# Apply stage of a split-precision block product: high and low columns in one 512-column matmul

## The reference

```python
h   = x @ weight.T + bias1 + scale[adapter] * (x @ A[adapter].T) @ B[adapter].T   # rank 16
Wq  = NF4[codes] * absmax           # one absmax per block of 64
out = x + h @ Wq.T + bias2
```

## Time and profile before

| | |
|---|---|
| median of 3 runs | 2300.09 us (2298.8 to 2300.9) |
| profiled execution, its own time | 2299.26 us |
| its span in the trace | 2297.5 us |
| PE busy, PEld busy | 2202.1 us (96%), 2009.1 us (87%) |
| DVE, ACT busy | 1707.1 us (74%), 1116.0 us (49%) |
| DMA, mean | 240 GB/s |
| apply stage, matmuls L1076, L1077, L1078 on comb,xs | 3584 each |

### The profile page before, as it was taken

The page is one execution under the profiler, slowest core; times in us unless marked ns, Lnnn a source line. Parts: engine busy times, 40 slices in busy tenths (PEclk is TensorE's granted clock), DMA queues, the critical chain, the costliest instruction groups (busy, mean ns, idle before and its releaser), DMA issues.

```text
span 2297.5 us, 37544 instructions
## 1 busy us (share of the span) xinstructions
PE 2202.1 (96%) x15082; PEld 2009.1 (87%) x15082; DVE 1707.1 (74%) x2434; ACT 1116.0 (49%) x1494; POOL 0.2 (0%) x4
## 2 busy tenths in 40 slices
PE   1489999999999999999999999999999999999999
PEld 1368877887788777899999999999999999999999
DVE  8988897897888565487777776676776676767665
ACT  6666665665666333354444443433444343443432
POOL 0000000000000000000000000000000000000000
PEclk9799999999999999999999999999999999999999
DMA  5248887887787898877777877777887777977775
GB/s 116 73 147 259 253 272 217 269 253 229 252 262 244 252 302 271 262 244 236 241 234 233 273 266 244 239 239 248 283 265 239 238 243 244 303 249 235 242 244 171
DMA packets 399331, 550.51 MB, mean 240 GB/s; under 512 B 41624, under 2 KB 256280, under 8 KB 399032
## 3 DMA queue, kind: packets, MB, share of 16 engines
q1 hardware_dynamic: 399160, 548.12, 76.0%
HBM read 421.66 MB, written 127.42 MB: 239 GB/s over the span
## 4 chain that ended last, share of the span: by engine, by line
PE 57%; DVE 0%; issue 0%; DVEq 0%
PE ps L1078 18%; PE ps L1076 18%; PE ps L1077 18%; PE ps L1119 1%; PE ps L1108 0%; DVE xs L870 0%; DVE res L949 0%; DVE res L927 0%; DVE res L942 0%; DVE low_st L887 0%; DVE low_rep L934 0%; DVEq L947 0%
## 5 line engine op out<-in xcount | busy, mean ns | idle before, releaser
L1076 PE MATMUL ps<-comb,xs 128*128 128x256 f32 (+1 forms) x3584 | 1014.6, 283 | 1.7 <-issue 1.0
L1078 PE MATMUL ps<-comb,xs 128*128 128x256 f32 (+1 forms) x3584 | 1014.6, 283 | 0.0
L1077 PE MATMUL ps<-comb,xs 128*128 128x256 f32 (+1 forms) x3584 | 1009.3, 282 | 0.0
L611 ACT CAST xs<-xr 128x1024 fp32r<-128x1024 f32 x427 | 448.1, 1051 | 633.2 <-DMA xr<-xc_d 632.7
L870 DVE TENSOR_TENSOR xs<-xr,xs 128x1024 fp32r<-128x1024 f32 x427 | 522.3, 1224 | 293.6 <-ACT xs L611 291.7
L1077 PEld LDWEIGHTS ps<-comb,xs 128*128 128x128 f32 x3584 | 677.8, 189 | 5.3
L1076 PEld LDWEIGHTS ps<-comb,xs 128*128 128x128 f32 x3584 | 676.6, 189 | 2.3 <-issue 1.4
L1078 PEld LDWEIGHTS ps<-comb,xs 128*128 128x128 f32 x3584 | 676.7, 189 | 0.0
L1076 PE MATMUL ps<-wq,tile 128*128 128x512 f32 x1088 | 476.1, 438 | 0.0
L1078 PE MATMUL ps<-wq,tile 128*128 128x512 f32 x1088 | 427.7, 393 | 0.0
L1077 PE MATMUL ps<-wq,tile 128*128 128x512 f32 x1088 | 426.7, 392 | 0.0
(11 more groups left out here) (99 smaller groups left out, 1720.2 us busy)
## 6 DMA issues: line engine op xcount, KB each, us to landing
xr<-xc_d SPq DMA_DIRECT2D x427, 512.0 KB, 4.0
raw<-in_L_cond_weight_dram SPq DMA_DIRECT2D x128, 512.0 KB, 4.6
xc_d<-rq SPq DMA_DIRECT2D x32, 1792.0 KB, 7.6
x_nat<-in_x_dram SPq DMA_DIRECT2D x128, 256.0 KB, 3.8
res<-in_x_dram SPq DMA_DIRECT2D x64, 512.0 KB, 5.4
out_dram<-res SPq DMA_DIRECT2D x128, 256.0 KB, 5.0
wc_d<-cs SPq DMA_DIRECT2D x32, 896.0 KB, 4.6
comb_raw<-wc_d SPq DMA_DIRECT2D x28, 1024.0 KB, 7.4
```

The source lines that it names most:

```text
L611: nc.scalar.copy(xs[f][:, HI, :, :], xr[f][:, LO, :, :]).then_inc(s_xhi, 1)
L1076: nc.tensor.matmul(out_ap, t_hi, m_hi, start=first, stop=False)
L1077: nc.tensor.matmul(out_ap, t_hi, m_lo, start=False, stop=False)
L1078: return nc.tensor.matmul(out_ap, t_lo, m_hi, start=False, stop=last)
```

## The change

A predicate is_wide(i) names the products that are done in another form. In strip 0 these are SS1, S4 and A22 of passes 0 to 14; in strips 1 to 3 all seven products, without those of the last pass of strips 1 and 2 and without the first two of each strip's first pass. (The last pass of strip 0 is out as well; the last of strip 3 is in.)

For such a product the high part of x is multiplied in one matmul with the high and the low columns of the weight block, 2x256 columns, into the whole bank. The low part of x is multiplied with the high columns as before, into the left half. So a step of k has two matmuls (512 and 256 columns) instead of three (256 each). In the last step the two change places, so that the 512-column matmul is the last of the product. The right half of the bank then holds x high by weight low, and DVE adds it in an instruction of its own ahead of the old one, with a wait of DVE for itself (s_evh) in between. The other products keep their form.

```diff
+    def is_wide(i):
+        pp, f = divmod(i, NF)
+        j, p = divmod(pp, PAIRS)
+        if p == PAIRS - 1 and j + 1 < NS:
+            return False
+        return f not in WITH_LOW if j == 0 else not (p == 0 and f < 2)
+
+    def wide_before(i):
+        return sum(is_wide(n) for n in range(i))
...
+                wide, n_wide = is_wide(i), wide_before(i) + 1
+                low_half = bank[:, HW:2 * HW]
                 if f == A11:
+                    if wide:
+                        tt(u_sum[:, :], low_half, u_sum[:, :], ALU.add).then_inc(s_evh, 1)
+                        dve.wait_ge(s_evh, n_wide)
                     tt(r[:, 0, 0, :], u_sum[:, :], r[:, 0, 0, :], ALU.add).then_inc(s_ev, 1)
...
                 elif f == SS1:
+                    if wide:
+                        tt(r[:, :, 1, :], low_half.unsqueeze(1).to_broadcast([P, 2, HW]), r[:, :, 1, :],
+                           ALU.add).then_inc(s_evh, 1)
+                        dve.wait_ge(s_evh, n_wide)
                     tt(r[:, :, 1, :], bank[:, 0:HW].unsqueeze(1).to_broadcast([P, 2, HW]), r[:, :, 1, :],
                        ALU.add).then_inc(s_ev, 1)
...
-                for k in range(HK):
+                if is_wide(i):
+                    for k in range(HK):
+                        x_hi, x_lo = xs[f][:, HI, k, :], xs[f][:, LO, k, :]
+                        both, high = cw[f][:, k, :, cols], cw[f][:, k, HI, cols]
+                        if k < HK - 1:
+                            nc.tensor.matmul(bank[:, :], x_hi, both, start=(k == 0), stop=False)
+                            nc.tensor.matmul(bank[:, 0:HW], x_lo, high, start=False, stop=False)
+                        else:
+                            nc.tensor.matmul(bank[:, 0:HW], x_lo, high, start=False, stop=False)
+                            last = nc.tensor.matmul(bank[:, :], x_hi, both, start=False, stop=True)
+                    last.then_inc(s_prod, 1)
+                for k in range(0 if is_wide(i) else HK):
                     last = three(psum, xs[f][:, HI, k, :], xs[f][:, LO, k, :], cw[f][:, k, HI, cols],
                                  cw[f][:, k, LO, cols], k == 0, k == HK - 1)
```

More of the change, by code:

```diff
@@ L264, in adaln_ffn_kernel @@
         s_ev = sem("product_added")
+        s_evh = sem("high_columns_of_wide_product_added")
         s_ab = sem("a_b_loaded")
@@ L918, in add_product @@
                         tt(spread(0), thrice(u_low[:, :]), thrice(bank[:, low]), ALU.add).then_inc(s_lrep, 1)
+                    if wide:
+                        tt(r[:, 0, 0, :], low_half, r[:, 0, 0, :], ALU.add).then_inc(s_evh, 1)
+                        dve.wait_ge(s_evh, n_wide)
                     tt(r[:, 0, 0, :], bank[:, main], r[:, 0, 0, :], ALU.add).then_inc(s_ev, 1)
@@ L939, in add_product @@
                 elif f == S4:
+                    if wide:
+                        tt(r[:, 0, 1, :], low_half, r[:, 0, 1, :], ALU.add).then_inc(s_evh, 1)
+                        dve.wait_ge(s_evh, n_wide)
                     tt(r[:, 0, 1, :], bank[:, 0:HW], r[:, 0, 1, :], ALU.add).then_inc(s_ev, 1)
                 else:
+                    if wide:
+                        tt(r[:, 1, 0, :], low_half, r[:, 1, 0, :], ALU.add).then_inc(s_evh, 1)
+                        dve.wait_ge(s_evh, n_wide)
                     tt(r[:, 1, 0, :], bank[:, 0:HW], r[:, 1, 0, :], ALU.add).then_inc(s_ev, 1)
@@ L1227, in _ @@
                 pe.wait_ge(s_xlo, split_of(i) + 1)
-                for k in range(HK):
+                if is_wide(i):
[10 more added lines that the diff above has]
+                for k in range(0 if is_wide(i) else HK):
                     last = three(psum, xs[f][:, HI, k, :], xs[f][:, LO, k, :], cw[f][:, k, HI, cols],
                                  cw[f][:, k, LO, cols], k == 0, k == HK - 1)
-                last.then_inc(s_prod, 1)
+                    if k == HK - 1:
+                        last.then_inc(s_prod, 1)
                 if j == 0 and f == 3:
```

## The result

The changed kernel takes 2285.83 us (median of 6 runs, 2283.67 to 2287.02), the kernel before 2299.64 us in the same comparison: a ratio of 0.9938, 95% interval 0.9928 to 0.9949. So it is faster by 14 us. 2271 us was forecast, with a range of 2264 to 2285: the direction was right, the size was twice too large, and the time lies just outside the range.

The account below looks back on a forecast made before the run. PE was taken to bound the apply stage, by number of matmuls times their distance. 2299.3 - 30.6 (PE steps) + 1.2 (strip starts) + 0.5 (end) = 2270.4, so 2271 us with the median's 0.8; range 2264 to 2285 us.

Parts of the forecast that it names:

- 226.7 + 118.7 = 345.4 ns: PE's step of k in wide products: one 512- and one 256-column matmul instead of 356.0 ns, saving 10.6 ns.
- The 118.7 ns: PE's distance for a 256-column matmul in the apply stage, worked out from a pass of 20.39 us.
- The end: After the last block matmul one more DVE add stands before L942: +0.5 us, all visible.
- DVE in mid-strip: DVE 86 to 90% busy in mid-strip, idle time ahead of L870 halved, at no cost to PE.
- The start of a strip: Late DVE adds at three strip starts: 0.5 us to spare before product 231; 0 to 6 us put, 1.2 taken.
- A: Rival: the dropped matmul was cheap, 512-column distance 230 to 235 ns, saving 7 to 21 us; 2281 to 2295 us; chance 0.08.
- A's sign: On PE, a 512-column distance over 232 ns would make the rival of the cheap dropped matmul true.
- a mean of 58 steps: End of the weight stage: 13.15 us / 58 = 226.7 ns, taken as the 512-column distance.
- B: Rival: PE waits for DVE at strip starts or x comes late, 4 to 8 us back each; 2280 to 2293; chance 0.09.
- C: Rival: DVE becomes the bound, a pass longer than 20.39 us, slower than before, for instance 2317 us; chance 0.04.
- D: Rival: the load was the true limit at 256 columns, so more gain than forecast, below 2265 us; chance 0.04.
- The rule of the Trainium skill: Matmul distance at full clock is columns / 2.4 plus 2.5 ns; one matmul less saves 2.5 ns a step, 7.2 us.

Follow-up runs that it names:

- e1: Changed kernel with high and low columns of A11, A12, S2, S3 side by side in one run of 512 in strips 1 to 3; 2287.39 us.
- e14: Changed kernel with x's low part also multiplied by both halves in wide products, so all 16 matmuls have 512 columns; 2592.57 us.
- e15: e14 with S4 and A22 blocks 64 bytes behind a multiple of 128, A11, A12, S2, S3 at one, in strips 1 to 3; 2590.69 us.
- e8: Kernel before, still three 256-column matmuls, with the compact layout of e1 in strips 1 to 3; 2310.66 us.
- e16: e6 with all weight blocks at multiples of 128 bytes and in one run in strips 1 to 3; 2278.68 us.
- e6: Changed kernel with the order of the 512- and 256-column matmuls turned around in every second step; 2280.04 us.
- e5: Changed kernel with the eight 512-column matmuls of a wide product first, then the eight of 256; 2281.73 us.
- e12: e6 with all weight blocks but SS1's 64 bytes behind a multiple of 128 in strips 1 to 3, columns in one run; 2275.27 us.
- e4: Changed kernel without the added DVE adds and their waits, so x high by weight low is missing from its output; 2284.21 us.
- e9: Kernel before with the weight blocks of S4 and A22 placed 64 bytes lower in strips 1 to 3; 2294.04 us.
- e10: e8 with every buffer from 160 KB on placed 64 bytes higher, moving x of A11 and A12 alone among the seven products' operands; 2307.29 us.
- e13: e5 with all weight blocks but SS1's 64 bytes behind a multiple of 128 in strips 1 to 3; 2279.13 us.
- e7: e1 with each step of k keeping its old pitch of 576 words, 64 unused; 2288.37 us.

## Why the prediction was wrong

**The step that failed** is PE's price of a step after the change, "226.7 + 118.7 = 345.4 ns". It measured 351.1 ns. It adds two prices that were each read where nearly all neighbours have the same length, and takes for granted that they stay when the two lengths alternate. They don't.

e1 tests just this, without any question of place. There all operands begin at multiples of 128 bytes. Among their own kind the two lengths cost 226.7 ns (e14, e15) and 120.0 ns (e8) at that place, together 346.7 ns. In turn they took 351.7 ns, 5.0 ns more, nearly half of the 10.6 ns forecast as the gain. Read from start to start, with the mean over e1's passes, it is the long one that pays: about 235 ns in five of the seven products, and 117 ns for the short one. The order carries the cost: at the same places the mirrored order takes 348.2 ns (e16), and the changed kernel's 351.1 become 349.1 mirrored (e6) and 350.0 grouped (e5).

The place of the blocks is a second effect, and it can't simply be added. By prices among their own kind A11, A12, S2 and S3, 64 bytes off, should take 231.7 + 117.8 = 349.5 ns, the three others 226.7 + 119.6 = 346.3, in the mean 348.1. That would put 2.7 of the 5.7 missing ns down to the place. But e1 gave the four blocks the place where 512 columns are cheap, and nothing was gained: their steps went from 352.6 to 351.8 ns, those of the three others from 349.2 to 351.5. And e12, with six blocks at the dear place, needs 347.3 ns, less than the 349 that its own prices add up to. So prices by length and place predict streams of one length and not mixed ones. Why a mixed stream costs what it does isn't shown.

The 118.7 ns, read from whole passes, was a mean of 117.8 and 119.6, and hid that the products differ; a reading by product was to be had. It is not what made the sum wrong: three times it is 356.0 ns, and 355.8 was measured.

**What this makes.** Strips 1 to 3: 316 products are 45 passes; 0.26 us were gained in each instead of 0.59, 12 us instead of 27. Strip 0, where only SS1, S4 and A22 are wide: before, L1119 stands at 1034.29 and two passes later at 1076.97; in the changed kernel's chain of waits, L1155:

```profile
1035.09 0.23 PE ps L1155
...
1077.22 0.23 PE ps L1155
```

42.68 us became 42.13: 0.27 us a pass where 0.25 was forecast. In all 16 us on PE. Less 0.5 us at the end and 1.0 us in the first pass of the apply stage this is 14.3 us; the spans differ by 14.1.

**The first pass** was overlooked. The prediction looked for waits at the starts of strips 1 to 3; one came at the start of strip 0, where DVE makes the operand of a transposition ahead of the first LoRA matmul. Before, then changed kernel:

```profile
994.35 0.33 PE L1108 MATMUL ps<-ident,low_rep 128*128 128x128 f32 x1 [0.42 <-DVE low_rep L934]
995.39 0.33 PE L1144 MATMUL ps<-ident,low_rep 128*128 128x128 f32 x1 [1.19 <-DVE low_rep L961]
```

PE's wait grew by 0.8 us. In e4, without the added adds, it is 0.5 us, so the adds are the cause. With the 0.5 us at the end that is most of the 1.6 us by which e4 is faster.

**The end** was right: one more add, 0.46 us.

```profile
2278.73 0.40 PE L1273 MATMUL ps<-comb,xs 128*128 128x512 f32 x1
...
2279.17 0.42 DVE L976 TENSOR_TENSOR res<-ps,res 128x256 f32<-128x256 f32 x1 [1.37 <-PE ps L1273]
2279.63 0.42 DVE L978 TENSOR_TENSOR res<-ps,res 128x256 f32<-128x256 f32 x1
```

**DVE in mid-strip** was right: 85% where 86 to 90% was expected, and its idle time ahead of the low part of x fell from 54.5 us to 24.0 in the same window.

**The start of a strip** was right in its mechanism, and the 1.2 us allowed for it were not needed. DVE's adds of product 226, and the first matmuls of products 230 and 231 on PE:

```profile
1652.92 0.42 DVE L944 TENSOR_TENSOR u_sum<-ps,u_sum 128x256 f32<-128x256 f32 x1
1653.37 0.42 DVE L946 TENSOR_TENSOR u_sum<-ps,u_sum 128x256 f32<-128x256 f32 x1
1653.83 0.42 DVE L948 TENSOR_TENSOR res<-u_sum,res 128x256 f32<-128x256 f32 x1
```
```profile
1651.99 0.39 PE L1269 MATMUL ps<-comb,xs 128*128 128x512 f32 x1
...
1654.80 0.39 PE L1269 MATMUL ps<-comb,xs 128*128 128x512 f32 x1
```

The add ends at 1654.25 and product 231 begins at 1654.80: 0.55 us to spare, where 0.5 was worked out. Behind the first pass PE has no wait for DVE. The 0.8 us for L876 on the page, at 991 us, are in the kernel before as well.

**The rivals.** A, which was given a chance of 0.08, is what happened, in size (2281 to 2295) and in mechanism: "with the change from one length to the other" is in it. Its price, 230 to 235 ns for 512 columns, was read from L1119, the one row with a long matmul among short ones; the changed kernel's mean is 233.1 ns, over the 232 ns that the prediction named as A's sign. I had put L1119 down to the border of products, and preferred a mean of 58 steps that was exact but had no short matmul in it. Of B only the 0.8 us of the first pass came, C and D didn't. The rule of the Trainium skill named there (TensorE: Matmul & The Clock Gate, Back-to-back issue gap), which the page gives for single matmuls, would have given 7 us; the rows of e14 and e15, 226.7 ns at 512 columns for a rule of 215.8, disagree with it as those of before did.

## What to carry to other kernels

A price holds for the neighbours that it was read with. When a change mixes what stood apart, a row of the mixture, even a single one at a border, says more than an exact mean of either alone. Read prices by product before they are averaged: a distance of 118.7 ns was two, 117.8 and 119.6. When matmuls of two lengths alternate, try other orders and a shift of one operand by 64 bytes, and try them together: with the same instructions the order was worth 6 us, the shift nothing alone and 5 us on top of the order.

## What the runs showed of the hardware

Among matmuls of its own length, a float32r matmul with its own load took its columns and two units of 6.67 ns where both operands begin at multiples of 128 bytes from the common base: 120.0 ns for 256 (e8), 226.7 for 512 (e14, e15). With one of the two 64 bytes off it was mostly 117.8 ns for 256 (e9, e10, and 113 to 114 in two products of e13) and 231.7 to 233.4 ns for 512. 6.67 ns are 16 columns at 2.4 GHz, and 16 fp32 words are 64 bytes; that the load of one operand and the stream of the other meet in such pieces is an inference, not shown.

Among matmuls of the other length the long one took about 235 ns and the short one 117 (e1), and in groups of eight the long ones took 229.3 to 230.2 ns instead of 226.7 (SS1, S4, A22 in e5), in A22 falling from 236 to 226 within the group. In most kernels the step of a product repeats to the tenth of a nanosecond over passes; in e1 and e7 two products take 347.6 and 351.6 ns in turn. Steps don't move when DVE loses a sixth of its work (e4), so DVE's added work takes no part in them; for ScalarE and the DMA engines no run shows it.

It stays open why the long matmul is dearer in a mixed stream, why one product's steps depend on its neighbours (SS1 in e1, A11 in e9), and why the shift helps in the mirrored order alone.
